# A block-sparse ReLU layer in a twelve-layer decoder kernel: turns and output products laid between the chunks

## The chip, the cores and the metric

One core of a Trainium2 chip. The time is that of one execution of the whole program on the device, in microseconds (us); lower is better.

## The reference

The kernel computes four decoder layers of three blocks each, `x = x + block(layernorm(x))`, on 16 x 64 = 1024 rows of 512 numbers in float32. The change lies in one block, the feed-forward of layer 1:

```python
def _L1_ffn_ref(x, c1_w, c2_w, w1, w2t):   # DIM 512, INTER 1792, SPARSITY 32, RANK 16
    xf = x.reshape(B * T, M)
    inter = xf @ c1_w.T @ c2_w.T
    blk = inter.reshape(B * T, n_blocks, SPARSITY)
    idx = jnp.argmax(blk, axis=-1) + jnp.arange(0, INTER, SPARSITY)
    w1_g = w1[idx]
    w2_g = w2t[idx]
    h = jax.nn.relu(jnp.einsum('bkm,bm->bk', w1_g, xf))
    out = jnp.einsum('bk,bkm->bm', h, w2_g)
```

For each row and each of the 56 blocks of 32 inner columns, a low-rank product (rank 16) picks the one column with the highest score, the first if several are equal. Only this column's inner value passes, after a ReLU. The result goes through the second weights back to 512 columns.

## The kernel before

The program is a row of stages, one per block, with a barrier between them; each stage writes its five engines' lists by hand, with semaphores for every hand-over. Nothing is reordered by a scheduler: what `stage_l1_ffn` writes is the order on each engine. The stage's names in the profile begin with l1f.

The rows are cut into T = 8 tiles of 128. For a tile n the work is:

- ScalarE normalises the rows (`Front.norm`, L259) into `xn`; TensorE turns them (transposes, `Front.turn`, L265), four 128x128 turns into the PSUM bank `pt`; ScalarE copies the bank to `xT` (`Front.copy`, L270). This is done for tile n + 1 during tile n.
- Low-rank product (L2523): `xT` with the first low-rank weights into `pc`, which ScalarE copies to `low` (L2564).
- Four chunks of 448 inner columns. For each, TensorE makes the inner product `ph` (L2530, four products of 128 rows, each shown as two passes) and the scores `pi` (L2535, one product of 16 rows, two passes). `ph` and `pi` have two banks each. VectorE then finds the chosen column of each block of 32 in five operations on the scores (L2595 to L2606) and writes the masked ReLU into `h` (L2611), which sets `chunk_done`. TensorE may start chunk c when chunk c - 2 is done.
- Fourteen turns of `h` (L2545) in four groups of 4, 4, 4 and 2 (`groups`). ScalarE copies each group from the bank to `hT` (L2570).
- Fourteen output products (L2553, 28 passes of 512 columns) add up in `po`. ScalarE copies `po` to `ob` (L281), GpSimd adds it to `x` (L289), and VectorE measures the new rows for the next stage's norm (`Ahead`, L185 to L189).

On TensorE these stand one after the other: low-rank product, four chunks, the turns of the next tile's rows, all fourteen inner turns, all output products. All turns use the one bank `pt`, so that each group waits for the copy of the one before:

```python
                    for g, (a, b) in enumerate(groups):
                        pe.wait_ge(hT_ready, NG * n + g + 1)
                        pe.wait_ge(chunk_done, NCH1 * n + min(-(-b * P // CH1), NCH1) + 1)
```

The first wait is for the bank (copy of the group before), the second for the columns of `h` that the group turns. Groups 0 to 3 need chunks up to 1, 2, 3 and 3. `every_tile` unrolls the tiles. The second weights `w2` are loaded by SyncE at the stage's start (L2511), after the first weights' four parts.

Of the kernel before, what the change touches and what calls it, by code (L numbers as in the profile page):

```python
# [13 lines left out]
P = 128  # L14
D = 512
KC = D // P
B, S = 16, 64
T = B * S // P
# [23 lines left out]
def last(n):  # L42

    return isinstance(n, int) and n == T - 1
# [7 lines left out]
def every_tile(body):  # L52
    for n in range(T):
        body(n, n % 2)
# [11 lines left out]
class Stage:  # L66
    last = []
# [176 lines left out]
class Front(Norm):  # L244
# [32 lines left out]
    def out(self, act, n):  # L277

        act.wait_ge(self.out_ready, n + 2)
        act.wait_ge(self.added, n + 1)  # L280
        self.nc.scalar.copy(self.ob[:, :], self.po[:, :]).then_inc(self.out_copied, 1)  # L281
# [2187 lines left out]
NCH1, CH1 = 4, INTER1 // 4  # L2469
HC1 = INTER1 // P  # L2470


def stage_l1_ffn(nc, m, w_c1, w_c2, w_1, w_2):

    st = Stage(nc, "l1f")
    with st:
        wc1 = st.sb("wc1", [P, KC, LOW1])
        wc2 = st.sb("wc2", [LOW1, INTER1])
        w1 = st.sb("w1", [P, KC, INTER1])
        w2 = st.sb("w2", [P, HC1, D])  # L2480
        ramp = st.sb("ramp", [P, BLOCK1])
        f = Front(nc, st, m)
        ahead = Ahead(nc, st, m)
        low = st.sb("low", [LOW1, P])
# [5 lines left out]
        h = st.sb("h", [P, INTER1])  # L2490
        hT = st.sb("hT", [P, HC1, P])
        pc = st.ps("pc", [P, 512])
        pi = st.ps("pi", [P, 2, 512])
        ph = st.ps("ph", [P, 2, 512])
        loaded, down_loaded = st.dma_sem("loaded"), st.dma_sem("down_loaded")
# [5 lines left out]
        NG = len(groups)  # L2501
        st.begin()
        with nc.Block() as block:
# [13 lines left out]

            @block.tensor
            def _(pe):
                def body(n, u):  # L2520
                    pe.wait_ge(f.xT_ready, n + 2)
                    for k in range(KC):
                        mm = pe.matmul(pc[0:LOW1, 0:P], wc1[:, k, :], f.xT[:, u, k, :], start=k == 0, stop=k == KC - 1)  # L2523
                    mm.then_inc(low_ready, 1)
                    for c in range(NCH1):
                        pe.wait_ge(chunk_done, NCH1 * n + c if c else NCH1 * n + 1)
                        if n == 0:
                            pe.wait_ge(w1_loaded[c], 16)
                        for k in range(KC):
                            mm = pe.matmul(ph[:, c % 2, 0:CH1], f.xT[:, u, k, :], w1[:, k, c * CH1:(c + 1) * CH1],  # L2530
                                           start=k == 0, stop=k == KC - 1)
                        mm.then_inc(hid_ready, 1)
                        if c == 0:
                            pe.wait_ge(low_copied, n + 2)
                        pe.matmul(pi[:, c % 2, 0:CH1], low[:, :], wc2[:, c * CH1:(c + 1) * CH1],  # L2535
                                  start=True, stop=True).then_inc(score_ready, 1)
                    if not last(n):
                        pe.wait_ge(hT_ready, NG * n + 1)
                        f.turn(pe, n + 1)
                    pe.wait_ge(f.xT_ready, n + 2 if last(n) else n + 3)  # L2540
                    for g, (a, b) in enumerate(groups):
                        pe.wait_ge(hT_ready, NG * n + g + 1)
                        pe.wait_ge(chunk_done, NCH1 * n + min(-(-b * P // CH1), NCH1) + 1)
                        for j in range(a, b):
                            mm = pe.transpose(f.pt[:, (j - a) * P:(j - a + 1) * P], h[:, j * P:(j + 1) * P], m.ident[:, :])  # L2545
                        mm.then_inc(h_turned, 1)
                    if n == 0:
                        pe.wait_ge(down_loaded, 16)
                    pe.wait_ge(f.out_copied, n + 1)
                    for g, (a, b) in enumerate(groups):  # L2550
                        pe.wait_ge(hT_ready, NG * n + g + 2)
                        for j in range(a, b):
                            mm = pe.matmul(f.po[:, :], hT[:, j, :], w2[:, j, :], start=j == 0, stop=j == HC1 - 1)  # L2553
                    mm.then_inc(f.out_ready, 1)

                f.turn(pe, 0)
                pe.wait_ge(loaded, 32)
                every_tile(body)

            @block.scalar  # L2560
            def _(act):
                def body(n, u):
                    act.wait_ge(low_ready, n + 2)
                    nc.scalar.copy(low[:, :], pc[0:LOW1, 0:P]).then_inc(low_copied, 1)  # L2564
                    if not last(n):
                        f.act(act, n + 1, 1 - u)
                    for g, (a, b) in enumerate(groups):
                        act.wait_ge(h_turned, NG * n + g + 2)
                        act.wait_ge(f.out_ready, n + 1)
                        nc.scalar.copy(hT[:, a:b, :], f.pt[:, 0:(b - a) * P].rearrange("p (k t) -> p k t", t=P)) \  # L2570
                            .then_inc(hT_ready, 1)
                    f.out(act, n)

                f.act(act, 0, 0)
                every_tile(body)

            @block.vector
            def _(dve):
# [1498 lines left out]
```

## Time and profile before

| | us |
|---|---|
| median of 3 runs (4424.14 to 4428.93) | 4424.42 |
| the profiled execution's own time | 4423.18 |
| its span in the trace | 4421.3 |
| TensorE busy | 4036.8 |
| VectorE busy | 2180.9 |
| ScalarE busy | 1427.2 |
| mean granted TensorE clock | 0.946 |

The span runs from the first to the last instruction in the trace; the own time is the device time of that same execution. Busy time of TensorE is that of its matmul records, which are pipelined and end where a model puts them. PEld is TensorE's loading of weights, beside the matmuls. The granted clock is a share of 2.4 GHz. In rows in order of time, "[0.68 <-ACT ...]" is idle time of the engine before the row and what ended it.

### The profile page before, as it was taken

Reading aid. Unit: us, or ns where it says so; the run is one execution under the profiler, and the core shown is the slowest. Engines: PE = TensorE matmul, PEld = TensorE weight load, DVE = VectorE, ACT = ScalarE, POOL = GpSimd, SP = SyncE. Lnnn points to the kernel's source line nnn. Section 1 sums busy time; section 2 is a strip of 40 time slices with the busy share of each in tenths; the row PEclk is TensorE's granted clock in tenths of the full one; section 3 lists DMA queues with packets and bytes.
Section 4 is the critical chain, followed back from the end, with each engine's and each line's share of the span. In section 5 each row is a group of like instructions: output and inputs, shape, how many; then the busy total and the mean of one; then the engine's idle time right before and its main releaser. Section 6 shows DMA issues by size and latency. Waiting matters only on the chain. (4 is left out here: it accounts for less than half of the span.)

```text
span 4421.3 us, 52019 instructions
## 1 busy us (share of the span) xinstructions
PE 4036.8 (91%) x19210; PEld 2182.2 (49%) x19210; DVE 2180.9 (49%) x3809; ACT 1427.2 (32%) x2603; POOL 312.6 (7%) x288
## 2 busy tenths in 40 slices
PE   8899989998788999998988779699999999999997
PEld 3334434554365555544446564355555455555554
DVE  0777665553256322334438428766546454344433
ACT  3776755453133211111113234212112133222232
POOL 1011001211002000000000011000000000000000
PEclk9999999999888999998988889899999999999998
DMA  4111121111002322201000021200000011111100
GB/s 176 55 55 36 58 89 36 39 34 46 0 25 101 124 96 106 94 15 68 0 26 1 39 97 36 67 31 22 20 25 34 1 64 34 34 34 35 46 26 22
DMA packets 133915, 215.11 MB, mean 49 GB/s; under 512 B 42704, under 2 KB 95056, under 8 KB 123072
## 3 DMA queue, kind: packets, MB, share of 16 engines
q1 hardware_dynamic: 133696, 212.06, 13.7%
q8 instruction: 153, 2.51, 0.2%
q14 instruction: 66, 0.54, 0.0%
HBM read 167.99 MB, written 44.04 MB: 48 GB/s over the span
## 5 line engine op out<-in xcount | busy, mean ns | idle before, releaser
L810 PE MATMUL l3x_pj<-kvT,l3x_wq 128*128 128x512 f32 x512 | 232.8, 609 | 3.7 <-issue 3.7
L810 PE MATMUL l3a_pj<-kvT,l3a_wq 128*128 128x512 f32 x512 | 228.0, 599 | 7.7 <-issue 7.7
L908 PE MATMUL l3a_po<-l3a_wo,l3a_cT 128*128 128x512 f32 x512 | 230.5, 603 | 2.5 <-ACT l3a_cT L1037 2.1
L432 PE MATMUL l1x_pj<-kvT,l1x_wq 128*128 128x512 f32 x512 | 228.3, 599 | 0.7 <-ACT kvT L240 0.7
L477 PE MATMUL l1x_po<-l1x_wo,l1x_cT 128*128 128x512 f32 x512 | 226.2, 596 | 1.2 <-issue 1.2
L573 DVE TENSOR_TENSOR x<-x,l1x_po 128x512 f32<-128x512 f32 x64 | 44.1, 689 | 266.9 <-PE l1x_po L477 266.9
L810 PEld LDWEIGHTS l3x_pj<-kvT,l3x_wq 128*128 128x128 f32 x512 | 98.2, 196 | 119.8 <-issue 119.8
L810 PEld LDWEIGHTS l3a_pj<-kvT,l3a_wq 128*128 128x128 f32 x512 | 96.7, 193 | 121.4 <-issue 121.3
L908 PEld LDWEIGHTS l3a_po<-l3a_wo,l3a_cT 128*128 128x128 f32 x512 | 95.5, 191 | 120.7 <-issue 111.0
L477 PEld LDWEIGHTS l1x_po<-l1x_wo,l1x_cT 128*128 128x128 f32 x512 | 95.7, 192 | 110.9 <-issue 110.9
L432 PEld LDWEIGHTS l1x_pj<-kvT,l1x_wq 128*128 128x128 f32 x512 | 94.6, 190 | 110.2 <-issue 107.2
L194 POOL TENSOR_TENSOR norm_rstd<-norm_half,minus_half 128x1 f32<-128x1 f32 x70 | 42.2, 604 | 1413.7 <-DVE norm_half L189 1413.7
L908 PE MATMUL l3x_po<-l3x_wo,l3x_cT 128*128 128x512 f32 x256 | 121.7, 620 | 4.2 <-ACT l3x_rq L1014 3.6
L908 PE MATMUL l3x_pc<-l3x_wo,l3x_cT 128*128 128x512 f32 x256 | 115.1, 592 | 0.0
L1167 DVE TENSOR_TENSOR x<-x,l3a_po 128x512 f32<-128x512 f32 x56 | 38.5, 687 | 154.8 <-PE l3a_po L908 154.8
L1593 ACT ACTIVATE l0a_signs<-l0a_lowest_a,l0a_scalars 128x1376 uint16<-128x1376 uint16 x68 | 98.0, 1441 | 49.9 <-DVE l0a_lowest_a L1716 49.2
L527 ACT COPY l1x_cT<-l1x_pa 128x512 f32<-128x512 f32 x64 | 34.4, 589 | 238.4 <-PE l1x_pa L466 238.4
L2553 PE MATMUL l1f_po<-l1f_w,l1f_hT 128*128 128x512 f32 x224 | 110.0, 653 | 0.0
L1466 PE MATMUL l0a_pg<-kvT,l0a_wk 128*128 128x512 f32 x192 | 90.8, 626 | 20.1 <-DMA l0a_wk<-in_L_xattn_Wk 10.2
L2530 PE MATMUL l1f_ph<-l1f_w,l1f_xT 128*128 128x448 f32 x256 | 106.4, 559 | 1.2 <-DMA l1f_w<-in_L_ffn_w 1.2
L1701 DVE TENSOR_SCALAR_CACHE_REDUCE l0a_keep<-l0a_keep,l0a_scalars 128x1376 uint16<-128x1376 uint16 x64 | 105.4, 1646 | 3.2 <-DVE l0a_scalars L1707 1.1
L1446 PE MATMUL l0a_pg<-l0a_wg,l0a_xT 128*128 128x512 f32 (+1 forms) x192 | 83.8, 597 | 24.3 <-issue 15.3
(521 smaller groups left out, 7815.4 us busy)
## 6 DMA issues: line engine op xcount, KB each, us to landing
l1x_kb<-l1x_keys SPq DMA_DIRECT2D x32, 512.0 KB, 4.6
l1x_vb<-l1x_values SPq DMA_DIRECT2D x32, 512.0 KB, 3.3
l1x_keys<-l0a_kv SPq DMA_DIRECT2D x48, 256.0 KB, 2.0
l1x_values<-l0a_kv SPq DMA_DIRECT2D x40, 256.0 KB, 2.3
kvT<-in_L_xattn_Wv SPq DMA_DIRECT2D x8, 1024.0 KB, 5.6
l1x_wq<-in_L_xattn_Wq SPq DMA_DIRECT2D x8, 1024.0 KB, 4.9
l1x_sbias<-in_L_xattn_bias SPq DMA_DIRECT2D x8, 1024.0 KB, 7.3
l1x_wo<-in_L_xattn_Wo SPq DMA_DIRECT2D x8, 1024.0 KB, 5.6
```

Of the source, the lines that this page charges most:

```text
L194: self.nc.gpsimd.tensor_tensor(self.rstd[:, t:t + 1], self.half[:, t:t + 1], self.m.minus_half[:, 0:1], ALU.pow).then_inc(self.root_ready, 1)
L432: mm = pe.matmul(pj[:, j, :], wq[:, u, k, h * DH:(h + 1) * DH], m.kvT[:, k, 1, 512 * j:512 * (j + 1)], start=k == 0, stop=k == KC - 1)
L477: mm = pe.matmul(po[:, t % 2, :], cT[:, u, h, t * P:(t + 1) * P], wo[:, u, h, :], start=h == 0, stop=h == GH - 1)
L573: nc.vector.tensor_tensor(m.x[:, t, :], m.x[:, t, :], po[:, t % 2, :], ALU.add).then_inc(added, 1)
L810: mm = pe.matmul(pj[:, j, :], wq[:, u, k, h * DH:(h + 1) * DH], m.kvT[:, k, 1, 512 * j:512 * (j + 1)], start=k == 0, stop=k == KC - 1)
L908: mm = pe.matmul(outs[t % 2][:, :], cT[:, h, t * P:(t + 1) * P], wo[:, u, h, :], start=h == 0, stop=h == GH - 1)
L1446: mm = pe.matmul(dst[:, c, 0:k], f.xT[:, n % 2, kc, :], w[:, kc, o:o + k], start=kc == 0, stop=kc == KC - 1)
L1466: mm = pe.matmul(banks[b], wk[:, k, h * DH:(h + 1) * DH], m.kvT[:, k, 0, 512 * j:512 * (j + 1)], start=k == 0, stop=k == KC - 1)
L1593: ins = nc.scalar.activation(signs[:, :], words, ACT.Sign, bias=at[:, :], scale=-1.0, accum_out=total[:, :])
L1701: nc.vector.tensor_scalar(below, words, found[:, :], 0.0, ALU.is_lt, ALU.add, accum_out=cnt[:, :]).then_inc(link, step.next())
L2530: mm = pe.matmul(ph[:, c % 2, 0:CH1], f.xT[:, u, k, :], w1[:, k, c * CH1:(c + 1) * CH1], start=k == 0, stop=k == KC - 1)
L2553: mm = pe.matmul(f.po[:, :], hT[:, j, :], w2[:, j, :], start=j == 0, stop=j == HC1 - 1)
```

## The change

Tile by tile, TensorE's list gets a new order: chunk 0, chunk 1, the turns of the next tile's rows, chunk 2, inner turns 0, chunk 3, output block 0, inner turns 1 and 2, output block 1, inner turns 3, the low-rank product of the next tile, output blocks 2 and 3. An output block g is the products whose inner rows group g has turned (4, 4, 4 and 2 products); all still add up in `po`. The stage gets a second PSUM bank `pt2`; inner groups 1 and 3 go there, 0 and 2 stay in `pt`, and a group waits for the copy of the one two before it in the same bank. On ScalarE the copy of the low-rank product moves behind the inner copies of the tile before. The other engines' lists stay as they are.

The diff in full:

```diff
--- before.py
+++ after.py
@@ -2490,6 +2490,7 @@
         h = st.sb("h", [P, INTER1])
         hT = st.sb("hT", [P, HC1, P])
         pc = st.ps("pc", [P, 512])
+        turned = [f.pt, st.ps("pt2", [P, 512])]
         pi = st.ps("pi", [P, 2, 512])
         ph = st.ps("ph", [P, 2, 512])
         loaded, down_loaded = st.dma_sem("loaded"), st.dma_sem("down_loaded")
@@ -2517,62 +2518,91 @@
 
             @block.tensor
             def _(pe):
-                def body(n, u):
+                def lowered(n, u):
                     pe.wait_ge(f.xT_ready, n + 2)
                     for k in range(KC):
                         mm = pe.matmul(pc[0:LOW1, 0:P], wc1[:, k, :], f.xT[:, u, k, :], start=k == 0, stop=k == KC - 1)
                     mm.then_inc(low_ready, 1)
-                    for c in range(NCH1):
-                        pe.wait_ge(chunk_done, NCH1 * n + c if c else NCH1 * n + 1)
+
+                def chunk(n, u, c):
+                    pe.wait_ge(chunk_done, NCH1 * n + c if c else NCH1 * n + 1)
+                    if n == 0:
+                        pe.wait_ge(w1_loaded[c], 16)
+                    for k in range(KC):
+                        mm = pe.matmul(ph[:, c % 2, 0:CH1], f.xT[:, u, k, :], w1[:, k, c * CH1:(c + 1) * CH1],
+                                       start=k == 0, stop=k == KC - 1)
+                    mm.then_inc(hid_ready, 1)
+                    if c == 0:
+                        pe.wait_ge(low_copied, n + 2)
+                    pe.matmul(pi[:, c % 2, 0:CH1], low[:, :], wc2[:, c * CH1:(c + 1) * CH1],
+                              start=True, stop=True).then_inc(score_ready, 1)
+
+                def hidden_turn(n, g):
+
+                    a, b = groups[g]
+                    if g == 0:
+                        pe.wait_ge(f.xT_ready, min(n + 3, T + 1))
+                    else:
+                        pe.wait_ge(hT_ready, NG * n + g if g > 1 else NG * n + 1)
+                    pe.wait_ge(chunk_done, NCH1 * n + min(-(-b * P // CH1), NCH1) + 1)
+                    for j in range(a, b):
+                        mm = pe.transpose(turned[g % 2][:, (j - a) * P:(j - a + 1) * P], h[:, j * P:(j + 1) * P], m.ident[:, :])
+                    mm.then_inc(h_turned, 1)
+
+                def out(n, g):
+                    a, b = groups[g]
+                    if g == 0:
                         if n == 0:
-                            pe.wait_ge(w1_loaded[c], 16)
-                        for k in range(KC):
-                            mm = pe.matmul(ph[:, c % 2, 0:CH1], f.xT[:, u, k, :], w1[:, k, c * CH1:(c + 1) * CH1],
-                                           start=k == 0, stop=k == KC - 1)
-                        mm.then_inc(hid_ready, 1)
-                        if c == 0:
-                            pe.wait_ge(low_copied, n + 2)
-                        pe.matmul(pi[:, c % 2, 0:CH1], low[:, :], wc2[:, c * CH1:(c + 1) * CH1],
-                                  start=True, stop=True).then_inc(score_ready, 1)
-                    if not last(n):
-                        pe.wait_ge(hT_ready, NG * n + 1)
-                        f.turn(pe, n + 1)
-                    pe.wait_ge(f.xT_ready, n + 2 if last(n) else n + 3)
-                    for g, (a, b) in enumerate(groups):
-                        pe.wait_ge(hT_ready, NG * n + g + 1)
-                        pe.wait_ge(chunk_done, NCH1 * n + min(-(-b * P // CH1), NCH1) + 1)
-                        for j in range(a, b):
-                            mm = pe.transpose(f.pt[:, (j - a) * P:(j - a + 1) * P], h[:, j * P:(j + 1) * P], m.ident[:, :])
-                        mm.then_inc(h_turned, 1)
-                    if n == 0:
-                        pe.wait_ge(down_loaded, 16)
-                    pe.wait_ge(f.out_copied, n + 1)
-                    for g, (a, b) in enumerate(groups):
-                        pe.wait_ge(hT_ready, NG * n + g + 2)
-                        for j in range(a, b):
-                            mm = pe.matmul(f.po[:, :], hT[:, j, :], w2[:, j, :], start=j == 0, stop=j == HC1 - 1)
-                    mm.then_inc(f.out_ready, 1)
+                            pe.wait_ge(down_loaded, 16)
+                        pe.wait_ge(f.out_copied, n + 1)
+                    pe.wait_ge(hT_ready, NG * n + g + 2)
+                    for j in range(a, b):
+                        mm = pe.matmul(f.po[:, :], hT[:, j, :], w2[:, j, :], start=j == 0, stop=j == HC1 - 1)
+                    if g == NG - 1:
+                        mm.then_inc(f.out_ready, 1)
 
                 f.turn(pe, 0)
                 pe.wait_ge(loaded, 32)
-                every_tile(body)
+                lowered(0, 0)
+                for n in range(T):
+                    u = n % 2
+                    chunk(n, u, 0)
+                    chunk(n, u, 1)
+                    if n + 1 < T:
+                        pe.wait_ge(hT_ready, NG * n if n else 1)
+                        f.turn(pe, n + 1)
+                    chunk(n, u, 2)
+                    hidden_turn(n, 0)
+                    chunk(n, u, 3)
+                    out(n, 0)
+                    hidden_turn(n, 1)
+                    hidden_turn(n, 2)
+                    out(n, 1)
+                    hidden_turn(n, 3)
+                    if n + 1 < T:
+                        lowered(n + 1, 1 - u)
+                    out(n, 2)
+                    out(n, 3)
 
             @block.scalar
             def _(act):
-                def body(n, u):
+                def low_copy(n):
                     act.wait_ge(low_ready, n + 2)
                     nc.scalar.copy(low[:, :], pc[0:LOW1, 0:P]).then_inc(low_copied, 1)
-                    if not last(n):
-                        f.act(act, n + 1, 1 - u)
+
+                f.act(act, 0, 0)
+                low_copy(0)
+                for n in range(T):
+                    if n + 1 < T:
+                        f.act(act, n + 1, 1 - n % 2)
                     for g, (a, b) in enumerate(groups):
                         act.wait_ge(h_turned, NG * n + g + 2)
                         act.wait_ge(f.out_ready, n + 1)
-                        nc.scalar.copy(hT[:, a:b, :], f.pt[:, 0:(b - a) * P].rearrange("p (k t) -> p k t", t=P)) \
+                        nc.scalar.copy(hT[:, a:b, :], turned[g % 2][:, 0:(b - a) * P].rearrange("p (k t) -> p k t", t=P)) \
                             .then_inc(hT_ready, 1)
+                    if n + 1 < T:
+                        low_copy(n + 1)
                     f.out(act, n)
-
-                f.act(act, 0, 0)
-                every_tile(body)
 
             @block.vector
             def _(dve):
```

TensorE's list in the program before, one tile (tile 1 begins with such a row; `pc` is the low-rank product, `ph` and `pi` a chunk and its scores, `pt<-ident,l1f_xn` turns of the next tile's rows, `pt<-ident,l1f_h` inner turns, `po` output products):

```order
L2523 MATMUL l1f_pc<-l1f_xT,l1f_wc1 16x128 x4
L2530 MATMUL l1f_ph<-l1f_w1,l1f_xT 128x448 x4
L2535 MATMUL l1f_pi<-l1f_wc2,l1f_low 128x448
L2530 MATMUL l1f_ph<-l1f_w1,l1f_xT 128x448 x4
L2535 MATMUL l1f_pi<-l1f_wc2,l1f_low 128x448
L2530 MATMUL l1f_ph<-l1f_w1,l1f_xT 128x448 x4
L2535 MATMUL l1f_pi<-l1f_wc2,l1f_low 128x448
L2530 MATMUL l1f_ph<-l1f_w1,l1f_xT 128x448 x4
L2535 MATMUL l1f_pi<-l1f_wc2,l1f_low 128x448
L265 MATMUL l1f_pt<-ident,l1f_xn 128x128 x4
L2545 MATMUL l1f_pt<-ident,l1f_h 128x128 x14
L2553 MATMUL l1f_po<-l1f_w2,l1f_hT 128x512 x14
```

The eighteen turns stand in a row behind the last chunk, and the products of the output behind all of them.

TensorE's list of the changed program, the same tile from its third chunk on:

```order
L265 MATMUL l1f_pt<-ident,l1f_xn 128x128 x4
L2532 MATMUL l1f_ph<-l1f_w1,l1f_xT 128x448 x4
L2537 MATMUL l1f_pi<-l1f_wc2,l1f_low 128x448
L2549 MATMUL l1f_pt<-ident,l1f_h 128x128 x4
L2532 MATMUL l1f_ph<-l1f_w1,l1f_xT 128x448 x4
L2537 MATMUL l1f_pi<-l1f_wc2,l1f_low 128x448
L2560 MATMUL l1f_po<-l1f_w2,l1f_hT 128x512 x4
L2549 MATMUL l1f_pt2<-ident,l1f_h 128x128 x4
L2549 MATMUL l1f_pt<-ident,l1f_h 128x128 x4
L2560 MATMUL l1f_po<-l1f_w2,l1f_hT 128x512 x4
L2549 MATMUL l1f_pt2<-ident,l1f_h 128x128 x2
L2524 MATMUL l1f_pc<-l1f_xT,l1f_wc1 16x128 x4
```

No more than eight turns stand in a row now, in two banks, and six output products follow the last row shown.

ScalarE's list of the changed program around a tile's end (`hT` copies of inner turns, `low` copy of the low-rank product, `ob` copy of the output, `xn` and `xT` the rows of the tile after):

```order
L2601 COPY l1f_hT<-l1f_pt 128x512 x3
L2601 COPY l1f_hT<-l1f_pt 128x256
L2591 COPY l1f_low<-l1f_pc 16x128
L281 COPY l1f_ob<-l1f_po 128x512
L259 ACTIVATE l1f_xn<-x,norm_shift,norm_rstd 128x512
L270 COPY l1f_xT<-l1f_pt 128x512
```

Before, the copy to `low` stood behind the copy to `ob`; the two have changed places. (Buffer numbers are left out in this list: two of the four copies to `hT` read the second bank.)

## Rows read from the trace of the kernel before

**Rows 1.** The page: the span, and busy time of each engine.

```profile
span 4421.3 us, 52019 instructions
...
PE 4036.8 (91%) x19210; PEld 2182.2 (49%) x19210; DVE 2180.9 (49%) x3809; ACT 1427.2 (32%) x2603; POOL 312.6 (7%) x288
...
```

**Rows 2.** Busy time, tile by tile: stretch, length, PE busy (count), granted clock, DMA share, GB/s.

```profile
...
1992.12:2033.48 41.36, 37.42 (x94) 0.84 0.44 176
2033.48:2071.04 37.56, 34.86 (x95) 0.91 0.00 0
...
2108.59:2147.91 39.32, 36.45 (x95) 0.87 0.00 1
...
2261.91:2299.56 37.65, 34.02 (x91) 0.91 0.00 1
...
```

**Rows 3.** TensorE in order of time (start, length, line, count): tile 0's end, tile 1.

```profile
...
2013.51 0.66 PE L265 MATMUL l1f_pt<-ident,l1f_xn 128*128 128x128 f32 x4
...
2033.48 1.05 PE L2523 MATMUL l1f_pc<-l1f_xT,l1f_wc 128*16 128x128 f32 x8
2034.46 3.27 PE L2530 MATMUL l1f_ph<-l1f_w,l1f_xT 128*128 128x448 f32 x8
2037.66 1.01 PE L2535 MATMUL l1f_pi<-l1f_wc,l1f_low 16*128 16x448 f32 x2
...
2051.08 0.66 PE L265 MATMUL l1f_pt<-ident,l1f_xn 128*128 128x128 f32 x4
2052.41 0.66 PE L2545 MATMUL l1f_pt<-ident,l1f_h 128*128 128x128 f32 x4 [0.68 <-ACT l1f_xT L270]
...
2057.81 13.30 PE L2553 MATMUL l1f_po<-l1f_w,l1f_hT 128*128 128x512 f32 x28
2071.04 1.05 PE L2523 MATMUL l1f_pc<-l1f_xT,l1f_wc 128*16 128x128 f32 x8
...
```

**Rows 4.** Groups of instructions in the stage: busy, mean ns, idle before and its releasers.

```profile
...
L2545 PE MATMUL l1f_pt<-ident,l1f_h 128*128 128x128 f32 x112 | 27.2, 379 | 23.1 <-ACT l1f_hT L2570 13.5 <-DVE l1f_h L2611 4.9 <-ACT l1f_xT L270 4.7
...
```

**Rows 5.** Busy time and granted clock of one microsecond in tile 1's turns.

```profile
...
2053.00:2054.00 1.00, 0.33 (x2) 0.62 0.00 0
...
```

**Rows 6.** A weight load among tile 3's output products at full clock.

```profile
...
2139.24 0.19 PEld L2553 LDWEIGHTS l1f_po<-l1f_w,l1f_hT 128*128 128x128 f32 x1 [0.24 <-issue]
...
```

**Rows 7.** All engines in order of time: ScalarE's and VectorE's work, start of tile 3.

```profile
...
2108.70 0.59 ACT L281 COPY l1f_ob<-l1f_po 128x512 f32<-128x512 f32 x1 [12.72 <-PE l1f_po L2553]
...
2109.84 0.81 ACT L259 ACTIVATE l1f_xn<-x,norm_shift,norm_rstd 128x512 f32<-128x512 f32 x1
...
2112.78 1.01 PE L2535 MATMUL l1f_pi<-l1f_wc,l1f_low 16*128 16x448 f32 x2
...
2113.83 0.62 DVE L2595 TENSOR_REDUCE l1f_best<-l1f_pi 128x14 f32<-128x448 f32 x1 [20.06 <-PE l1f_pi L2535]
...
2117.21 0.63 DVE L2611 SCALAR_TENSOR_TENSOR l1f_h<-l1f_ph,l1f_hit 128x448 f32<-128x448 f32 x1
...
2117.98 0.62 DVE L2595 TENSOR_REDUCE l1f_best<-l1f_pi 128x14 f32<-128x448 f32 x1
...
```

**Rows 8.** TensorE in order of time, stage l0x: turns of four between products.

```profile
...
1002.67 0.60 PE L2179 MATMUL l0x_pt<-ident,l0x_ke 128*128 128x128 f32 x4
1003.20 1.13 PE L2148 MATMUL l0x_pj<-l0x_cx,l0x_wk 64*128 64x512 f32 x4
...
1009.78 3.70 PE L1971 MATMUL l0x_fill<-kvT,l0x_fill_wk 128*128 128x512 f32 x8
1013.32 0.60 PE L2179 MATMUL l0x_pt<-ident,l0x_ke 128*128 128x128 f32 x4
...
```

**Rows 9.** The load of the second weights: issue, and us to landing.

```profile
...
L2511 SPq DMA_DIRECT2D l1f_w<-in_L_ffn_w2t x1: 1500/1500/1500, 1992.8 to 1992.8; - x1
...
DMA to landing us min/median/max: 18.1/18.1/18.1
```

**Rows 10.** Busy time and granted clock of two stretches, in stages l0x and l2x.

```profile
...
1000.00:1030.00 30.00, 30.00 (x147) 1.00 0.07 27
2551.81:2557.09 5.28, 3.16 (x17) 1.00 0.01 2
...
```

## The prediction

> **What bounds the kernel now.** I read the page first: the profiled execution spans 4421.3 us and TensorE is busy for 91% of it [rows 1]. The change touches one stage, the block-sparse layer (names l1f), so next I cut that stage into its eight tiles, from one low-rank product (L2523) to the next. The first takes 41.4 us, since it begins with its loads, the others 37.6 to 39.3, with TensorE's records on for some 93% of the time and a mean granted clock of 0.87 to 0.91 [rows 2]. The stage is 307.4 us long (1992.12 to 2299.56), 7% of the span, so all that can be won is here.
>
> Then I read one tile in order of time [rows 3]. Low-rank product to first chunk: 0.98 us. The four chunks run from 2034.46 to 2051.08, 16.62 us, without a gap of note. Then come the turns: the four of the next tile's rows, and after them the 14 of the inner rows in four groups. All go through one bank, so each group waits until ScalarE has copied the bank of the last one. From one group's start to the next is 1.33 us at full clock (2051.08 to 2052.41), of which 0.68 is idle. Over the stage the group of inner turns shows 23.1 us idle, most of it for the copy, a fifth for VectorE's h [rows 4]. From 2051.08 to 2057.81 TensorE makes 18 turns and no product: 6.73 us. In the middle of this the granted clock falls from 1.00 to 0.50, that is from 2.4 to 1.2 GHz: 0.62 in the microsecond 2053 to 2054 [rows 5]. What TensorE did before the fall was turns and waits only, since 2051.08. A mean of 0.91 over 37.56 us is 6.8 us at half. The output products (28 passes) start under the half clock and take 13.23 us to the next tile's low-rank product (2057.81 to 2071.04); at full clock a pass comes every 0.19 + 0.24 = 0.43 us [rows 6], so 28 take 12.0.
>
> VectorE is the hidden second bound: a chunk's scores start on TensorE at 2112.78, VectorE starts 1.05 us later, and its sixth operation ends at 2117.84, 4.01 us on; the next chunk's chain follows 0.14 later [rows 7]. That is 4.15 us a chunk beside TensorE's 4.15. So the last chunk's h comes about 5 us after its scores begin, and turns that need it can wait.
>
> **The change part by part.** Nothing is computed more or less: the same 18 turns, 28 output passes, 4 chunks and one low-rank product a tile. Only order, one bank and some waits change.
>
> (a) *New order on TensorE.* I lay the tile out by durations at full clock. Chunks: 4.15 us each (16.62 / 4). A block of four turns to whatever follows: 0.53 us at 1002.67 [rows 8]; I take 0.55. Two turns: half of 0.43 plus 0.11 for the switch, 0.33. A block of eight passes 128x512 to a block of turns: 3.54 us (1009.78 to 1013.32) [rows 8]; three of these and a last one of four passes (4 x 0.43 + 0.11 = 1.83) are 12.45. Low-rank product: 0.98. Sum of TensorE's work: 16.62 + 4 x 0.55 + 0.33 + 12.45 + 0.98 = 32.58 us.
>
> (b) *Waits left over.* Times from the tile's first chunk: chunk 1 at 4.15, turns of the next tile's rows at 8.32, chunk 2 at 8.87. Chunk 2 needs chunk 0's h, ready at 3.20 + 1.05 + 4.01 = 8.26 (3.20 is chunk start to scores, 2034.46 to 2037.66): no wait. Inner turns 0 at 13.03 need chunk 1's h, ready at 12.42: no wait, though only 0.6 us in hand. Chunk 3 at 13.58, output block 0 at 17.73, turns 1 at 21.27, turns 2 at 21.82. These need chunk 3's h, ready at 13.58 + 8.26 = 21.84, seen some 0.05 later: 0.08 us of wait. Output block 1 needs the copy of turns 1: 21.27 + 1.33 = 22.60, against 22.45: 0.15 us. Blocks 2 and 3 find their copies long made. So 0.23 us of waits a tile, in place of the 23.1 us that the stage shows before its inner turns [rows 4]. A tile is 32.58 + 0.23 = 32.81 us.
>
> (c) *Second bank.* It is what lets turns 2 follow turns 1 without the copy. With one bank turns 2 would start at 22.60 at the earliest, 0.7 us a tile.
>
> (d) *Low-rank product one tile early.* It still costs 0.98 us; its copy and its hand-over lie under output blocks 2 and 3. On ScalarE it now stands before the output copy, which waits for block 3 anyway; nothing is behind it. Cost nothing; uncovered it would be under 1 us a tile.
>
> (e) *ScalarE, GpSimd, VectorE.* The norm of the next tile's rows follows the last output copy at the tile's start and must be there at 8.32; the two take 0.59 and 0.81 us [rows 7]. GpSimd and VectorE keep their lists. Nothing here is on the path.
>
> (f) *The second weights' load in tile 0.* It is issued at 1992.8 and lands 18.1 us later, with 1.5 us of issuing at the outside 2012.4 [rows 9]. Tile 0's chunks end at 2013.51 now [rows 3]; in the new order output block 0 stands before the last inner turns, and after 1.1 us of added turns: 2014.6. A margin of 2.2 us; if the load were 3 us late the loss is 1 us once.
>
> (g) *Clock.* The turns are now in pieces of 0.55, 0.55, 1.33 (with the wait) and 0.33 us, with products between. Does the clock still fall? Where turns of four lie between products, from 1000 to 1030 us, the clock is 1.00 throughout [rows 8, 10]. A harder case: from 2551.81 to 2557.09 TensorE is on for only 3.16 of 5.28 us, in small products, turns and gaps, and the clock stays 1.00 [rows 10]. I take it to stay up here. The Trainium skill, TensorE: Matmul & The Clock Gate, Part 4 (PE-mode transpose), says that a transpose does not count as busy work for the clock; this trace agrees where turns stand in a row, and shows no fall where they are spread. By that rule taken alone the densest place, turns 1 and 2 with their waits, would be the one to trip, and the sum would be that of the first rival.
>
> *Sum.* Tile 0 and a tile like it: 37.56 - 32.81 = 4.75 us. Tiles 1 to 6, from 2033.48 to 2261.91, are 228.43 us [rows 2]; 6 x 32.81 = 196.86; saved 31.6. The last tile has no next rows to turn: 32.81 - 0.55 = 32.26 against 37.65, saved 5.4. Together 41.8 us. The profiled execution took 4423.18 us, 1.24 under the median of 4424.42 (its span 4421.3 lies 1.9 below its own time). 4423.18 - 41.8 = 4381.4, so 4382.6 for the median: **4383 us**.
>
> *Bounds.* The switch between blocks is 0.10 us at the least (3.54 less 8 x 0.43) and 0.19 at the most (a chunk's eight passes, 3.20 less 8 x 0.43 x 448/512); I took 0.11 as the turns' neighbours show. At 0.19 for nine blocks a tile is 0.7 us longer, 5.8 in all. Where a fall of the clock lies costs differently from tile to tile (37.56 against 39.32 [rows 2]), and every later stage now meets its own falls some 42 us earlier; three such differences either way are 5 us. That gives 4377 to 4394 for this case.
>
> **The rivals.**
> *One fall a tile remains.* The clock falls after turns 1 and 2 and comes back during block 2. For: today's fall begins within 3 us of the last product. Against: the longest piece without a product is now 1.33 us instead of 6.73. Price: 6.8 us at half hold 3.4 us less work; 8 x 3.4 = 27.2 given back, 41.8 - 27.2 = 14.6 saved, 4410 us.
> *Slower: the clock falls twice a tile.* The place is again TensorE, after chunk 1 with its turns and after turns 1 to 3 with the low-rank product; each fall costs 3.4 us. Two give back 54.4 us: 12.6 slower, 4437 us. It decides from 41.8 / 27.2 = 1.5 falls a tile on. Against it is the stretch of 30 us at 1.00 [rows 10]. The Trainium skill, same page, section A second HAM failure mode: psum-queue depth-cycling, tells that small idles between groups of products that go through banks in turn made the clock swing back and forth; that speaks against this change, and by it the time would be this rival's. The row from 2551.81 on does not bear it out.
> *The waits only move.* VectorE's 4.15 us a chunk leaves 0.6 us in hand at turns 0 and nothing at turns 2. If its chain ends 1 to 1.5 us later than I laid out, chunk 3, turns 2 and block 1 each wait: some 1.5 us a tile, 12 in all, 4395 us.
> *It does nothing*: the order stands as written, but TensorE is bound by something the rows don't show. Then 4424 us. The 23.1 us idle and the half clock are both in the rows, so I give it little.
>
> **How the numbers follow.** About 0.2% (9 us) is what a measurement of this kernel can tell from no change. Forecast, full clock and 0.2 us of waits a tile: 0.80. One fall a tile: 0.10. Waits move: 0.05. No change: 0.02. Two falls: 0.03. Faster is 0.95, within 0.2% is 0.02, slower 0.03. The range reaches from just under the first case's low end, 4375, over the moved waits to 4402, and leaves out the one-fall case, no change and two falls, 0.15, and little of the forecast's tails.
>
> **What would show it.** In the changed profile: tiles of 32.8 us (32 to 33.5) from low-rank product to low-rank product; granted clock 1.00 in each tile from the second to the seventh; idle before the inner turns under 3 us in the stage instead of 23.1, almost all for VectorE's h; output blocks at 3.5 us each, the sum of products unchanged in count; the stage's last product ending some 42 us earlier, and the later stages as long as now within a few us. Wrong would be: a clock of 0.9 in the tiles (first rival), tiles over 38 us (second), idle before chunk 3 or turns 2 above 1 us a tile (third), or the gain given back by a later stage.

## The result and the profile after

| | before | after |
|---|---|---|
| median, us | 4426.68 (4 runs, 4424.14 to 4431.15) | 4379.64 (4 runs, 4369.40 to 4383.26) |
| profiled execution, own time | 4423.18 | 4379.11 |
| its span | 4421.3 | 4377.3 |
| mean granted clock | 0.946 | 0.951 |

The ratio is 0.989, with a 95% interval of 0.9876 to 0.9904. The forecast was 4383; the time is 3.4 us below it, and the gain 47.0 us where 41.8 was forecast. The page after has as many instructions as before [rows 1]:

```profile
span 4377.3 us, 52019 instructions
...
```

To see where the time went, the span is cut by stages, from a stage's first matmul to the next stage's first: two of thirteen stretches, l1f and l3a (length, busy time of TensorE, granted clock, DMA share, GB/s). Before:

```profile
...
1990.00:2305.10 315.10, 283.74 (x752) 0.89 0.07 25
2865.70:3544.10 678.40, 655.12 (x3073) 0.98 0.07 26
...
```

After:

```profile
...
1986.80:2255.50 268.70, 259.13 (x753) 0.99 0.08 30
2819.00:3499.60 680.60, 656.82 (x3073) 0.98 0.07 26
...
```

The changed stage, the first row of each, went from 315.1 to 268.7 us, 46.4 less, with its clock from 0.89 to 0.99. Of the 46.4 us, TensorE's busy time gives 24.6 (283.74 less 259.13), though it does the same work, and its idle time 21.8. So about half of the gain is work that no longer runs at half clock, and about half is waits that are gone. Nobody touched the others: l0a is 3.1 shorter (626.1 against 629.2), l2f 3.2 longer (253.9 against 250.7) and l3a 2.2 longer, the rest within 1 us. All together make the 44.0 us by which the spans differ. So the page alone gives the gain of this edit only within some us, and the experiments below are read by the stage.

Tiles 0 and 1 after, here from first chunk to first chunk, since the low-rank product now stands elsewhere (answers to [rows 2]):

```profile
...
1991.80:2025.81 34.01, 33.88 (x95) 0.95 0.44 182
2025.81:2057.98 32.17, 32.04 (x96) 1.00 0.00 0
...
```

Tile 1 in order of time on TensorE (answers to [rows 3]):

```profile
...
2025.81 3.17 PE L2532 MATMUL l1f_ph<-l1f_w,l1f_xT 128*128 128x448 f32 x8
...
2029.85 3.27 PE L2532 MATMUL l1f_ph<-l1f_w,l1f_xT 128*128 128x448 f32 x8
...
2034.00 0.66 PE L265 MATMUL l1f_pt<-ident,l1f_xn 128*128 128x128 f32 x4
2034.49 3.17 PE L2532 MATMUL l1f_ph<-l1f_w,l1f_xT 128*128 128x448 f32 x8
...
2038.54 0.66 PE L2549 MATMUL l1f_pt<-ident,l1f_h 128*128 128x128 f32 x4
...
2043.08 3.70 PE L2560 MATMUL l1f_po<-l1f_w,l1f_hT 128*128 128x512 f32 x8
2046.62 1.36 PE L2549 MATMUL l1f_pt<-ident,l1f_h 128*128 128x128 f32 x8
2047.89 3.70 PE L2560 MATMUL l1f_po<-l1f_w,l1f_hT 128*128 128x512 f32 x8
2051.43 0.38 PE L2549 MATMUL l1f_pt<-ident,l1f_h 128*128 128x128 f32 x2
2051.74 1.05 PE L2524 MATMUL l1f_pc<-l1f_xT,l1f_wc 128*16 128x128 f32 x8
2052.72 5.42 PE L2560 MATMUL l1f_po<-l1f_w,l1f_hT 128*128 128x512 f32 x12
2057.98 3.17 PE L2532 MATMUL l1f_ph<-l1f_w,l1f_xT 128*128 128x448 f32 x8
...
```

The 18 turns stand in four places, each behind products; the longest stretch without a product is 1.27 us (2046.62 to 2047.89), where it was 6.73. The clock is 1.00 in all tiles that follow tile 0. Of the six between the first and the last, five take 32.17 us and tile 3 takes 32.34, against 37.56 to 39.32 before. The group of inner turns (answers to [rows 4]) has nearly no idle time left:

```profile
...
L2549 PE MATMUL l1f_pt<-ident,l1f_h 128*128 128x128 f32 x112 | 18.1, 278 | 1.4 <-DVE l1f_h L2641 0.5
...
```

23.1 us of idle became 1.4, and a turn takes 278 ns in the mean where it took 379, since none runs at half clock.

### The profile page after: what moved, and what is told of

Same layout as the page of the kernel before. It is cut to its first block and busy times, and to the rows that moved or that the text cites. A ratio compares the mean times of both kernels' runs of the same rounds, so it can differ in the third digit from the quotient of the medians.

```text
span 4377.3 us, 52019 instructions
## 1 busy us (share of the span) xinstructions
PE 4017.6 (92%) x19210; PEld 2174.5 (50%) x19210; DVE 2180.6 (50%) x3809; ACT 1428.1 (33%) x2603; POOL 312.9 (7%) x288
## 5 line engine op out<-in xcount | busy, mean ns | idle before, releaser
L810 PE MATMUL l3a_pj<-kvT,l3a_wq 128*128 128x512 f32 x512 | 228.5, 600 | 7.9 <-issue 7.9
L810 PE MATMUL l3x_pj<-kvT,l3x_wq 128*128 128x512 f32 x512 | 229.8, 603 | 3.6 <-issue 3.6
L810 PEld LDWEIGHTS l3a_pj<-kvT,l3a_wq 128*128 128x128 f32 x512 | 96.7, 192 | 122.1 <-issue 122.0
L810 PEld LDWEIGHTS l3x_pj<-kvT,l3x_wq 128*128 128x128 f32 x512 | 97.1, 193 | 117.9 <-issue 117.9
```

Source lines behind the costliest of these rows:

```text
L810: mm = pe.matmul(pj[:, j, :], wq[:, u, k, h * DH:(h + 1) * DH], m.kvT[:, k, 1, 512 * j:512 * (j + 1)], start=k == 0, stop=k == KC - 1)
```

## The experiments

All are read by the stage's length (before 315.1, changed 268.7 us) and by its tiles. A tile is from chunk 0 to chunk 0.

**The second bank alone, in the old order.** Inner turns 1 and 3 go to the new bank; TensorE's order is that of the kernel before.

```diff
+        turned = [f.pt, st.ps("pt2", [P, 512])]
...
-                        pe.wait_ge(hT_ready, NG * n + g + 1)
+                        pe.wait_ge(hT_ready, NG * n + g if g > 1 else NG * n + 1)
...
```

(and the inner turns and their copies use `turned[g % 2]` in place of `f.pt`.)

> The kernel before with nothing but the second bank: inner turns 1 and 3 go to it, the order on TensorE stays. My theory (the order is what counts, since without it TensorE runs out of products while VectorE makes the last h): turns 2 still wait for chunk 3's h, about 4.1 us after the turns begin (scores of chunk 3 at 2050.14, +1.05 +4.01), so the stretch without products goes from 6.73 us only to about 5.0 to 5.4, the clock still falls in it (0.90 to 0.93 a tile), a tile is 36 to 36.7 us against 37.6, the stage 8 to 14 us shorter than before. Rival (the waits for the one bank are what costs): the stretch shrinks to about 3.5 us, the clock stays up, a tile is 33 to 34.5 us and the stage 28 us shorter or more.

Measured: stage 294.5 us, 20.6 less than before; median 4401.87, ratio 0.9951 (0.9934 to 0.9967). Three of its tiles:

```profile
...
2030.03:2064.70 34.67, 32.15 (x96) 1.00 0.00 0
2064.70:2101.05 36.35, 33.83 (x96) 0.95 0.00 0
2101.05:2137.77 36.72, 33.85 (x96) 0.95 0.00 1
...
```

The turns of the first of these:

```profile
...
2047.99 1.09 PE L2546 MATMUL l1f_pt<-ident,l1f_h 128*128 128x128 f32 x8 [0.68 <-ACT l1f_xT L270]
2050.92 0.85 PE L2546 MATMUL l1f_pt<-ident,l1f_h 128*128 128x128 f32 x6 [1.84 <-DVE l1f_h L2612]
2051.61 12.18 PE L2554 MATMUL l1f_po<-l1f_w,l1f_hT 128*128 128x512 f32 x28
...
```

Neither theory had it. The wait for VectorE's h is there as I said (1.84 us before turns 2, the two last groups in one row of six turns), and the stretch without products is 5.0 us. But the clock fell in only two of the six tiles after tile 0, and in the last one: a tile is 34.67 us where it holds and 36.35 or 36.72 where it falls. The waits are hardly shorter, 2.52 us a tile in place of 2.70, but the stretch that holds them is (5.0 us in place of 6.7), and with that the clock holds in most tiles. A fall costs 1.7 to 2.1 us here, with 3.4 us at half clock. In tile 1 of the kernel before it was 6.8 us at half; that tile took 37.56 us with 0.2 us more of waits than the 34.67 here, so that by an estimate the fall cost about 2.7 us there.

**The new order with one bank.**

```diff
-        turned = [f.pt, st.ps("pt2", [P, 512])]
+        turned = [f.pt, f.pt]
...
-                        pe.wait_ge(hT_ready, NG * n + g if g > 1 else NG * n + 1)
+                        pe.wait_ge(hT_ready, NG * n + g + 1)
...
-                        pe.wait_ge(hT_ready, NG * n if n else 1)
+                        pe.wait_ge(hT_ready, NG * n + 1)
```

> The changed kernel with all turns in the one bank again, order as changed. My theory: only turns 2 must wait for the copy of turns 1, 1.33 us after the start of turns 1 in place of 0.65; a tile is 32.6 to 32.8 us against 32.17, the stage 4 to 5 us longer than with two banks, clock 1.00. Rival (the two banks matter): turns 1 to output block 1 become a stretch of over 1.8 us without products, the clock falls in some tiles, and the stage is 15 us longer or more.

Measured: stage 271.8 us, ratio 0.9888 (0.9872 to 0.9905), which overlaps the changed kernel's. All six tiles after tile 0 are alike:

```profile
...
2029.21:2061.77 32.56, 31.88 (x95) 1.00 0.00 0
...
```

```profile
...
2050.03 0.60 PE L2549 MATMUL l1f_pt<-ident,l1f_h 128*128 128x128 f32 x4
2051.30 0.66 PE L2549 MATMUL l1f_pt<-ident,l1f_h 128*128 128x128 f32 x4 [0.68 <-ACT l1f_hT L2601]
...
```

One wait of 0.68 us for the copy, no fall of the clock; 0.39 us a tile, 3.1 in the stage, a little under the 4 to 5 expected. The whole time does not show them: the median, 4377.53, is 2.1 us under the changed kernel's 4379.64. By the stage, the order alone brings 43.3 of the 46.4 us, and the bank adds 3.1 to it, though the bank alone brings 20.6 to the old order. The two parts remove the same waits.

**The low-rank product back at its own tile's start.**

```diff
-                lowered(0, 0)
                 for n in range(T):
                     u = n % 2
+                    lowered(n, u)
...
-                    if n + 1 < T:
-                        lowered(n + 1, 1 - u)
```

(and `low_copy(n)` first in ScalarE's tile.)

> The changed kernel with the low-rank product and its copy back at the start of their own tile. My theory: it costs the same 0.98 us there, its copy lies under chunk 0; the tile stays at 32.2 us and the stage within 1 us of the changed kernel's. Rival (the early place hides something): the scores of chunk 0 wait for the copy, and a tile is 0.3 to 1 us longer, the stage 2.4 to 8 us.

Measured in a single run (4370.60 us), the stage as one stretch:

```profile
...
1989.00:2257.50 268.50, 258.84 (x753) 0.99 0.08 29
...
```

268.5 against 268.7 us: where the changed kernel puts it, the low-rank product costs and brings nothing.

**Sixty-four turns more, in a row.**

```diff
                     out(n, 0)
+                    for j in range(64):
+                        pe.transpose(pc[:, P:2 * P], h[:, 0:P], m.ident[:, :])
                     hidden_turn(n, 1)
```

> The changed kernel with 64 more turns in a row behind output block 0 in each tile, into a part of a bank that nobody reads; the result is not changed. They take 64 x 0.107 = 6.8 us at full clock, as long as the stretch of turns and waits in the kernel before, but with no idle time in it. If it was the idle time that let the clock fall before (my theory): clock 1.00 in the tiles, a tile is 32.17 + 6.85 = 39.0 us, the stage 55 us longer. If turns don't count as work for the clock (rule of the Trainium skill, TensorE: Matmul & The Clock Gate, Part 4): the clock falls to half within or behind them in each tile, clock about 0.91, a tile is 41 to 43 us, the stage 70 to 85 us longer.

Measured in a single run (4434.60 us): stage 324.5 us, 55.8 longer. A tile, and the stretch in it:

```profile
...
2037.27:2076.42 39.15, 38.91 (x159) 1.00 0.00 0
...
```

```profile
...
2058.08 7.15 PE L2579 MATMUL l1f_pc<-ident,l1f_h 128*128 128x128 f32 x64
2065.07 1.04 PE L2549 MATMUL l1f_pt<-ident,l1f_h 128*128 128x128 f32 x8
2066.34 3.70 PE L2560 MATMUL l1f_po<-l1f_w,l1f_hT 128*128 128x512 f32 x8 [0.24 <-ACT l1f_hT L2603]
...
```

From 2058.08 to 2066.34, 8.26 us, TensorE makes 72 turns and no product, with 0.24 us idle, and the clock is 1.00 in every tile after tile 0. Turns without waits hold a clock that stands at 1.00.

**As long, with waits.** Five groups of four turns, each copied by ScalarE and waited for.

```diff
+                    for r in range(5):
+                        for j in range(4):
+                            mm = pe.transpose(pc[:, j * P:(j + 1) * P], h[:, 0:P], m.ident[:, :])
+                        mm.then_inc(x_turned, 1)
+                        pe.wait_ge(x_copied, 5 * n + r + 2)
                     hidden_turn(n, 1)
...
```

(and ScalarE copies each group to `dump`, a tile that nobody reads, before its copy of turns 1.)

> The changed kernel with five more groups of four turns behind output block 0 in each tile, each group into the bank of the low-rank product, copied by ScalarE to a tile that nobody reads, and waited for: the pattern of the kernel before, 5 x 1.33 = 6.7 us. The result is not changed. It stands beside the run with 64 turns in a row, as long but without waits, where the clock stayed at 1.00. Theory (idle time among turns lets the clock fall): it falls in each tile, clock 0.87 to 0.93, a tile is 40.5 to 43 us and the stage 65 to 85 us longer than the changed kernel's 268.7. Rival (it is not the waits but something else in the old order, such as the wait for VectorE or the length without chunks): clock 1.00, a tile 38.8 to 39 us, the stage 53 to 55 us longer.

Measured in a single run (4430.78 us): stage 333.8 us, 65.1 longer. A tile, and the stretch in the one before it (the clock falls in each of the six tiles between the first and the last; in this one only at the end of the five groups):

```profile
...
2073.76:2114.70 40.94, 37.56 (x116) 0.92 0.00 0
...
```

```profile
...
2055.76 0.66 PE L2582 MATMUL l1f_pc<-ident,l1f_h 128*128 128x128 f32 x4 [0.68 <-ACT l1f_dump L2609]
...
2061.08 1.89 PE L2551 MATMUL l1f_pt<-ident,l1f_h 128*128 128x128 f32 x8 [0.68 <-ACT l1f_dump L2609]
2062.79 4.59 PE L2562 MATMUL l1f_po<-l1f_w,l1f_hT 128*128 128x512 f32 x8
...
```

Eight turns that take 1.27 us in the changed kernel take 1.71 to the block behind them (2061.08 to 2062.79), and that block of eight passes 4.43 in place of 3.54. This is the old kernel's pattern put into the new order: same length as the 64 turns (8.31 us to the next product against 8.26), fewer turns, waits between them, and the clock falls in six tiles of eight, where it fell in none. With that run it shows that turns alone, or the lack of products alone, do not let it fall, and that waits among turns do.

They do not always. The first and the last tile have the same five groups with the same waits, and there the clock stays at 1.00 over the whole stretch, with 3.6 us idle in each:

```profile
...
2015.65:2023.59 7.94, 4.32 (x30) 1.00 0.00 0
2298.95:2306.88 7.93, 4.31 (x29) 1.00 0.00 0
...
```

In tile 1 of the kernel before, on the other hand, the clock falls right behind this stretch, which has 0.8 us idle:

```profile
...
2051.08:2053.20 2.12, 1.32 (x9) 1.00 0.00 0
...
```

So the sum of idle time does not order the cases, and what decides between them was not settled. Nor was it tried whether the same waits among products would do the same.

**The inner turns together again.** Two banks, the next rows' turns still between chunks; the fourteen inner turns behind chunk 3, the output blocks behind them.

```diff
-                    hidden_turn(n, 0)
                     chunk(n, u, 3)
-                    out(n, 0)
+                    hidden_turn(n, 0)
                     hidden_turn(n, 1)
                     hidden_turn(n, 2)
-                    out(n, 1)
                     hidden_turn(n, 3)
                     if n + 1 < T:
                         lowered(n + 1, 1 - u)
+                    out(n, 0)
+                    out(n, 1)
```

> The changed kernel with its two banks and the turns of the next rows between the chunks, but with all fourteen inner turns together behind chunk 3 and the output blocks behind them. By the durations of the changed kernel: chunks and turns end at 17.1 us, turns 0 and 1 take 1.0, turns 2 wait until chunk 3's h at 21.2 (some 3.1 us idle), turns 2 and 3 and the low-rank product end at 22.9, output 12.2: 35.1 us a tile at full clock against 32.17. Theory (idle time sets the clock, and 3.1 us in one piece is more than the 2.5 us that made it fall in two tiles of six with two banks in the old order): it falls in most tiles, 36.5 to 38 us a tile, the stage 35 to 45 us longer than the changed kernel's. Rival (spread of the next rows' turns is enough to keep the clock): clock 1.00, 35.1 us a tile, stage 24 us longer. Either way the gain of the change comes from inner turns and output blocks lying between chunks.

Measured: stage 310.5 us, 41.8 longer than the changed kernel's; median 4421.16, ratio 0.9985 (0.9973 to 0.9996).

```profile
...
2036.36:2073.78 37.42, 34.25 (x95) 0.91 0.00 0
...
```

```profile
...
2053.24 1.09 PE L2549 MATMUL l1f_pt<-ident,l1f_h 128*128 128x128 f32 x8
2057.51 1.51 PE L2549 MATMUL l1f_pt<-ident,l1f_h 128*128 128x128 f32 x6 [3.17 <-DVE l1f_h L2641]
...
2060.77 13.18 PE L2560 MATMUL l1f_po<-l1f_w,l1f_hT 128*128 128x512 f32 x28
...
```

3.17 us of idle in one piece, and the clock falls in each tile. Products between chunk 3 and turns 2 are what the change puts there: VectorE needs that time for the last h, and without them nearly the whole gain is gone, even with two banks. The stage is also 16.0 us longer than with two banks in the old order (294.5). There the next rows' turns and their copy lay in VectorE's time, and TensorE idled 2.52 us a tile; here they lie between chunks, it idles 3.17, and the clock falls in every tile.

**The low-rank product between turns 1 and turns 2.**

```diff
                     hidden_turn(n, 1)
+                    if n + 1 < T:
+                        lowered(n + 1, 1 - u)
                     hidden_turn(n, 2)
                     out(n, 1)
                     hidden_turn(n, 3)
-                    if n + 1 < T:
-                        lowered(n + 1, 1 - u)
```

(and ScalarE's copy to `low` behind that of turns 1.)

> The changed kernel with the next tile's low-rank product between turns 1 and turns 2, its copy behind that of turns 1. In the changed kernel turns 1, turns 2 and their hand-over take 1.28 us to output block 1, of which 0.98 is work. Theory (the 0.3 us is the wait for the copy of turns 1, covered by 0.98 us of low-rank product): a tile is 31.9 us, the stage 2 to 2.5 us shorter than 268.7; the whole time within the spread of the changed kernel's. Rival (turns 2 now stand before a shorter list and the copy to low delays the copy of turns 2, which output block 2 needs): the tile stays at 32.2 us or grows by 0.2.

Measured: median 4373.09, ratio 0.988 (0.9864 to 0.9897). A tile and the whole stage, then the place:

```profile
...
2026.86:2058.47 31.61, 31.61 (x95) 1.00 0.00 0
...
1988.60:2253.00 264.40, 256.17 (x753) 0.99 0.08 30
...
```

```profile
...
2047.66 0.60 PE L2549 MATMUL l1f_pt<-ident,l1f_h 128*128 128x128 f32 x4
2048.20 1.05 PE L2524 MATMUL l1f_pc<-l1f_xT,l1f_wc 128*16 128x128 f32 x8
2049.17 0.66 PE L2549 MATMUL l1f_pt<-ident,l1f_h 128*128 128x128 f32 x4
2049.66 3.60 PE L2560 MATMUL l1f_po<-l1f_w,l1f_hT 128*128 128x512 f32 x8
...
```

31.61 us a tile, with TensorE's records on all the time; the stage is 4.3 us shorter, twice the size expected. Turns 1, turns 2 and their switches take 0.54 + 0.49 = 1.03 us in place of 1.27: that is the wait for h and copy, 0.24. The other 0.3 lies in the shorter run from output block 1 to the next tile's chunk (8.81 us, 2049.66 to 2058.47, against 10.09 less the low-rank product's 0.98, 9.11).

**The two side by side.** Both kernels once more, on one chip.

> The changed kernel as it is, beside the next run on the same chip. Both theories: stage 268.7 us, ratio to the kernel before 0.987 to 0.991. How far the whole time spreads from run to run (4369 to 4383 in the first four) is what the next run must be read against.

> The kernel with the low-rank product between turns 1 and 2 again, now beside the changed kernel on one chip. Theory (its stage is 4.3 us shorter, 264.4 against 268.7, and nothing else changes): median 2 to 7 us under the changed kernel's, ranges overlapping. Rival (the 4.3 us are given back by where the clock falls in later stages): medians within 1 us or the other way round, with the stage still 264.4.

The changed kernel: 4383.25 us (4379.71 to 4386.66, 4 runs), ratio 0.9899 (0.9882 to 0.9915). The other: 4372.30 us (4366.28 to 4374.50, 4 runs), ratio 0.9878 (0.9862 to 0.9895). The ranges do not even meet here, though over both measurements of each they do (4369.40 to 4386.66 and 4366.28 to 4374.72). In the profiled executions, the stage and l3a, and a place in the changed kernel's l3a; changed kernel, then the other:

```profile
...
1994.40:2263.10 268.70, 259.18 (x752) 0.99 0.08 29
2825.60:3506.80 681.20, 657.20 (x3073) 0.98 0.07 26
...
3054.90 5.54 PE L810 MATMUL l3a_pj<-kvT,l3a_wq 128*128 128x512 f32 x9 [4.11 <-issue]
...
```

```profile
...
1991.00:2255.80 264.80, 256.42 (x753) 0.98 0.08 30
2815.50:3487.80 672.30, 652.64 (x3072) 0.98 0.07 26
...
```

The stage is 268.7 again, and 264.8. The other 7 of the 11 us between the medians were not expected; l3a alone, in which the kernels have the same instructions, differs by 8.9 us between these two executions. In it TensorE stands still at two places for something that no row names ("issue"): at both in the changed kernel's execution, 8.2 us in all, and at one in the other's, 3.5 us. So 4 us are shown as the version's own.

## Why the prediction was right, and where it was off

**The mechanism held.** The forecast case was turns between products, the waits gone and the clock at full speed, and the profile has all three. The reason given for the clock was only in part right, see (g).

**(a) The sum of the work** was too large: 32.81 us a tile with its waits, measured 32.17. In the tile above: chunks 4.04 and 4.15, and twice 4.05 behind a block of turns, 16.29 in place of 16.62; a block of four turns to what follows 0.49, not 0.55 (2034.00 to 2034.49); output blocks 3.54, 3.54 and 5.26 for the last two, 12.34 in place of 12.45. I took the chunk from a row where a score product stands before it, and a block of turns from a place with a 64-row product behind. These 0.64 us a tile make nearly all of the 4.6 us by which the forecast gain was short (41.8 against 46.4 in the stage): 3.7 in the six tiles between, where tile 3 gives 0.2 back, and some 0.4 each in the first and the last.

**(b) The waits left over** came where they were placed, and as small. VectorE's h of chunk 3 and ScalarE's copy of turns 1, beside the turns at 2046.62 (all engines, in order of time):

```profile
...
2046.58 0.62 DVE L2641 SCALAR_TENSOR_TENSOR l1f_h<-l1f_ph,l1f_hit 128x448 f32<-128x448 f32 x1
...
2047.26 0.59 ACT L2601 COPY l1f_hT<-l1f_pt 128x512 f32<-128x512 f32 x1 [7.43 <-PE l1f_pt L2549]
...
```

h ends at 2047.20, when turns 1 are just made, and output block 1 starts at 2047.89, 0.04 after the copy's end at 2047.85. Turns 1 and 2 to the block took 1.27 us; the forecast was 2 x 0.55 + 0.23 = 1.33. Tile 3 alone shows a wait for h before turns 2, 0.49 us. That is 0.5 of the 1.4 us idle before the inner turns in the stage, where "almost all" was forecast for h.

**(c) The second bank** was priced at 0.7 us a tile; the run with one bank measured 0.39: turns 1 and 2 take 1.76 us there in place of 1.27, and the output block behind them 0.10 less.

**(d) The low-rank product one tile early** was costed at nothing, and moving it back changed 0.2 us. That its place could be worth 0.56 us a tile, if it covers the wait of (b), I did not see.

**(e), (f) ScalarE and the load.** In tile 0 the first output block starts at 2010.91, right behind chunk 3, and over the stage the output products waited 0.0 us. Nothing was paid, as said.

**(g) The clock** was the step with the most at stake, and the reason given for it, that turns spread between products keep it, was right in its result but loose in its cause. The run with 64 turns shows that a row of turns without waits keeps the clock; the run with five waits shows that waits among turns can let it fall, in six tiles of eight. The Trainium skill, TensorE: Matmul & The Clock Gate, Part 4, says that transposes don't count as busy for the clock; here 8.26 us of float32 transposes with 0.24 us of idle kept it at 1.00 in all six tiles, so the measurement decides against that sentence for a clock that is already up. The prediction had read the old kernel's row of turns as agreeing with it; that row held 2.7 us of waits as well. The Trainium skill, TensorE: Matmul & The Clock Gate, A second HAM failure mode: psum-queue depth-cycling, blames small idles between groups that cycle through banks. The small idles agree with the old kernel (0.68 us between groups, a fall in each tile) and with the run with five waits; but how many banks the groups go through does not decide. The new order holds the clock with one bank and with two, and with the inner turns together the clock falls in each tile in spite of two banks. In the changed kernel such idles are nearly gone, and this rival did not come.

**The rivals.** One fall a tile and two falls a tile: the clock is 1.00, so neither. Their price, 3.4 us a fall, was high for the falls with two banks in the old order (1.7 to 2.1 us). Waits that only move: the wait before turns 2 is there, but 0.24 us with the copy and not 1.5. That nothing happens: the stage is 46.4 us shorter.

**The range** of 4375 to 4402 held the median; one of the first four runs (4369.40) lay below it. I had allowed 5 us either way for what other stages do by themselves; l3a alone differed by 12.8 us between profiled executions.

## What to carry to other kernels

Where a hand-written order has a stage in which the product engine waits for another engine several times in a row, first look for products that are already ready and put them between; more banks remove part of the same waits but cannot cover a wait for another engine's result. Count the waits twice: once as idle time, once as the time at half clock that may follow. In the kernel before, a tile had 2.7 us of idle, and by the estimate above its fall cost about as much again. And lay the shortest independent piece of work exactly where the last small wait is: the 0.98 us of low-rank product was free to move and was worth 4 us there.

## What was not expected of the hardware

- A fall of the clock is not a matter of having no products: 72 turns in 8.26 us kept it. Waits among turns let it fall, but no one number of these runs tells when: 0.68 us in one place a tile never did (new order, one bank); 2.52 us in a stretch of 5.0 (old order, two banks) did in two tiles of six, 3.4 to 3.6 us in a stretch of about 8 (five groups more) in six of eight, and 3.17 us in one piece in all eight; in the kernel before the clock fell in all eight, in tile 1 after 0.8 us of idle.
- The stages that nobody touched differ from execution to execution. In the profiled executions of these kernels l0a took 626.1 to 630.7 us and l3a 668.5 to 681.3. The kernel before itself ran from 4414.31 to 4430.10 in one set of seven. For l3a the traces show where: at two of its query products (L810) TensorE stands still for 3.5 to 4.2 us in some executions, each time with two transfers of the DMA queue "instruction" under way in it, and each time the clock falls to half towards its end or within 1.2 us behind it. In the execution of 668.5 us neither place stood still, in four (672.3 to 675.1 us) one did, in six (678.4 to 681.3 us) both. Why they stand still in one execution and not in another was not tried and stays open; an edit worth under 5 us can be judged only by its own stage.
